# A graph transformer layer on one core: the order of the first loads and of the last steps is changed, and ScalarE normalises the output blocks

## The reference

```python
k = decomp(x, node_type, comp_k, basis_k); q = ...; v = ...      # (n, 8 heads, 16)
kt = einsum('nhi,thij->tnhj', k, relation_att)[edge_type, src]
e = (q[dst] * kt).sum(-1) * relation_pri[edge_type] * 16 ** -0.5
a = softmax of e over the edges of each dst
vt = einsum('nhi,thij->tnhj', v, relation_msg)[edge_type, src]
agg = segment_sum(a[..., None] * vt, dst)
y = relu(decomp(agg, node_type, comp_a, basis_a) + x @ loop_weight + bias)
out = layernorm(x + y)
```

## Time and profile before

| what | us |
|---|---|
| median of 3 runs | 2042.28 |
| lowest, highest | 2038.15, 2045.23 |
| the profiled execution | 2054.15 |
| its span, first to last instruction | 2052.3 |

### The profile page before, as it was taken

One profiled execution on the slowest core, in us unless ns is written; L12 is line 12 of the kernel. 1 busy time (PEld: TensorE's weight loads), 2 busy tenths in 40 slices (PEclk: granted clock), 3 DMA queues, 4 the chain that ended last, 5 costly groups with the idle time before them and its releaser, 6 DMA issues.

```text
span 2052.3 us, 30216 instructions
## 1 busy us (share of the span) xinstructions
PE 1223.7 (60%) x6847; PEld 1015.7 (49%) x6848; DVE 1005.0 (49%) x2888; ACT 789.1 (38%) x2216; POOL 888.9 (43%) x927
## 2 busy tenths in 40 slices
PE   6999428565545555455564565555555455554788
PEld 3445215454445445455454554444544455444678
DVE  5866216444534445344453444434444344453777
ACT  4667216433333333333333333333333333333233
POOL 2781650444454444544445444354443544445000
PEclk9999759666777766777667667667776666667789
DMA  7787530222232222322223222232222322223113
GB/s 228 303 301 313 175 91 12 69 68 75 65 86 73 69 71 63 86 72 67 75 63 85 74 61 77 63 88 67 70 72 65 88 74 61 75 67 85 38 48 106
DMA packets 110628, 194.47 MB, mean 95 GB/s; under 512 B 24345, under 2 KB 76404, under 8 KB 104188
## 3 DMA queue, kind: packets, MB, share of 16 engines
q0 software_dynamic: 41680, 113.71, 19.6%
q1 hardware_dynamic: 66380, 79.10, 11.0%
q10 hardware_dynamic: 2400, 0.07, 0.1%
HBM read 134.12 MB, written 59.48 MB: 94 GB/s over the span
## 4 chain that ended last, share of the span: by engine, by line
another core or an unknown queue 30%; PE 26%; DVE 16%; issue 15%; DVEq 9%; ACT 2%; DMA 1%; ACTq 1%
PE pb L1703 6%; DVE agg L742 5%; PE pb L1651 4%; DVEq L713 4%; PE pb L1538 3%; DVE work L707 3%; PE pb L1813 2%; PE pb L1559 2%; PE pb L1678 2%; PE pb L1609 1%; DVE work L599 1%; PE pb L1640 1%; DVE work L609 1%; DVEq L582 1%
## 5 line engine op out<-in xcount | busy, mean ns | idle before, releaser
L1223 POOL DMA_INDIRECT kv<-table,idx_now x832 | 788.0, 947 | 935.0 <-DVE work L707 645.3
L742 DVE TENSOR_TENSOR agg<-agg,pb 128x136 f32 x832 | 241.8, 291 | 801.5 <-remote 613.8
L1703 PE MATMUL pb<-work,onehot 128*128 128x136 f32 x1664 | 391.6, 377 | 353.4 <-DVE agg L742 225.2
L1703 PEld LDWEIGHTS pb<-work,onehot 128*128 128x128 f32 x1664 | 327.0, 270 | 386.1 <-issue 244.9
L1365 ACT ACTIVATE work<-pb 128x512 f32<-128x512 f32 x208 | 123.9, 596 | 818.9 <-remote 636.6
L1651 PE MATMUL pb<-q_all,work 128*128 x1664 | 313.1, 351 | 0.1
L1651 PEld LDWEIGHTS pb<-q_all,work 128*128 128x128 f32 x1664 | 296.3, 265 | 3.7 <-issue 3.0
L1640 PE MATMUL pb<-ident,onehot 128*128 128x128 f32 x832 | 181.1, 357 | 184.3 <-ACT onehot L1359 99.9
L1352 ACT ACTIVATE work<-lane,neg_lane 128x128 f32<-128x128 f32 x800 | 252.9, 389 | 0.0
L1640 PEld LDWEIGHTS pb<-ident,onehot 128*128 128x128 f32 x832 | 127.6, 184 | 209.6 <-ACT onehot L1359 116.1
L599 DVE TENSOR_TENSOR work<-kv,pb 128x512 f32<-128x512 f32 x208 | 141.9, 682 | 22.0 <-issue 12.0
(11 more groups left out here) (202 smaller groups left out, 1291.4 us busy)
## 6 DMA issues: line engine op xcount, KB each, us to landing
table<-kv SPq DMA_DIRECT2D x49, 1024.0 KB, 4.7
kv<-table,idx_now POOLq DMA_INDIRECT x832
seg<-item_bias SPq DMA_DIRECT2D x52, 64.0 KB
kv<-base_rows SPq DMA_DIRECT2D x7, 448.0 KB, 4.5
kv<-in_x_dram SPq DMA_DIRECT2D x8, 384.0 KB, 5.7
pair<-in_x_dram SPq DMA_DIRECT2D x24, 128.0 KB
base_rows<-pair SPq DMA_DIRECT2D x24, 128.0 KB
onehot<-in_x_dram SPq DMA_DIRECT2D x7, 384.0 KB
```

What stands on the lines that cost most here:

```text
L742: v.tensor_tensor(a, a, PB[banks[i // 2 % len(banks)]][:, (i % 2) * 256:(i % 2) * 256 + W], ALU.add).then_inc(s_added, 1)
L1223: pool.indirect_dma_start(out=kv[:, o:o + 2 * D], out_offset=None, in_=table, in_offset=bass.IndirectOffsetOnAxis(ap=idx_now[par][:, i:i + ...
L1703: mm = t_.matmul(PB[banks[k % len(banks)]][:, u * 256:u * 256 + W], onehot[:, o:o + P], wv[:, b % WR, h * 2 + u, :], start=True, stop=True)
```

## The change

1. **First loads.** SyncE loads the k basis right behind x, ScalarE the v basis as its first instruction. The priorities come as one broadcast load, masked by head (`own_head`, three GpSimd operations) and summed on VectorE, in place of eight loads. GpSimd copies only the destinations first; sources and edge types follow once the bases have landed.
2. **Places in the table stage.** `STARTS_AT` 8 to 9, each column one block later, `QUERIES_AT` from block 45 to 41.
3. **Last group.** Each step of `maxima` stands ahead of two additions, not behind them; `weigh` of batches 2 to 7 is cut into four instructions that alternate with the additions.
4. **Layer stage.** All chunks but the last are normalised on ScalarE, between its copies; VectorE keeps reciprocal and shift, in the middle of `products3`.
5. **Last chunk.** Blocks 0 to 3, 4 and 5, and 6 as three parts, each with its own statistics and root; block 6 gets its own PSUM bank; three stores.

```diff
-        TILES_AT, STARTS_AT, BIAS_AT, QUERIES_AT = 4, 8, 24, BLOCKS - 4
-        COLUMNS_AT = [12, 13, 15, 16, 18, 19, 20]
+        TILES_AT, STARTS_AT, BIAS_AT, QUERIES_AT = 4, 9, 24, BLOCKS - 8
+        COLUMNS_AT = [13, 14, 16, 17, 19, 20, 21]
...
-                dve.wait_ge(s_relations_loaded, 16 * 3 * H)
+                dve.wait_ge(s_own_head, 3)
+                dve.wait_ge(s_relations_loaded, 16 * (2 * H + 1))
+                did(v.tensor_tensor(p3, p3, own_head.unsqueeze(1).broadcast_to([P, T, H]), ALU.mult))
+                did(v.tensor_reduce(pri, p3, AX.X, ALU.add))
...
             for k, steps in enumerate(maxima(g, 1, GROUPS // 2 - 1)):
+                steps()
                 late[2 * k]()
                 late[2 * k + 1]()
-                steps()
...
+                        if between and b == 1:
+                            between()
...
+            def inverse(ch):
                 dve.wait_ge(s_deviation, ch + 1)
                 v.reciprocal(rstd, rstd).then_inc(s_inverse_deviation, 1)
                 dve.wait_ge(s_inverse_deviation, ch + 1)
...
+                v.scalar_tensor_tensor(shift, mv[:, :, 0], -1.0, rstd, ALU.mult, ALU.mult).then_inc(s_shift, 1)
...
+            def stage3(ch, par, first=False):
+                products3(ch + 1, 1 - par, None if first else lambda: inverse(ch - 1))
                 residual(ch, par)
...
              x_chunk(0)
+            sp.dma_start(Bkv[:, :, 0, :], basis_k.rearrange("b (i o) -> i b o", o=D)).then_inc(s_bases_loaded, 16)
...
-            tile_load(0, dst)
-            tile_load(1, src)
-            tile_load(2, edge_type)
+            tile_load(0, dst, s_tile_rows)
...
+            pool.wait_ge(s_bases_loaded, 16 * 2)
+            tile_load(1, src, s_tile_more)
+            tile_load(2, edge_type, s_tile_more)
...
+            def normalise(ch, par, cs):
+                act.wait_ge(s_shift, ch + 1)
+                after(act, s_stored, ch, 16, 0)
+                for c in cs:
+                    a_.activation(yo[:, c * D:(c + 1) * D], y[par][:, c * D:(c + 1) * D], ACT.Identity,
+                                  bias=shift[:, c:c + 1], scale=rstd[:, c:c + 1]).then_inc(s_normalised, 1)
...
+                act.wait_ge(s_normalised, ch * CB)
+                root(0)
+                part(0)
+                root(1)
+                root(2)
+                part(1)
...
+            NORMS = {5: (0, 2), 6: (2, 4), CB: (4, CB)}
+            LAST_NORMS = {3: (0, 2), 4: (2, 4), 5: (4, CB)}
```

More of the change, by code:

```diff
@@ L173, in graph_transformer_layer @@
         pri = w1.take(T)
+        pri_all = w1.take(T * H)
+        own_head = w1.take(H)
         comp = w1.take(4 * NB, 96)
@@ L816, in _ @@
             for b in range(NBATCH):
-                merge(adding(g, range(2 * b, 2 * b + 2), LAST_SBANKS), [lambda: weigh(g, 1, b + 2)] if b + 2 < NBATCH else [])
+                merge(adding(g, range(2 * b, 2 * b + 2), LAST_SBANKS),
+                      [lambda u=u: weigh_item(g, 1, b + 2, u) for u in range(4)] if b + 2 < NBATCH else [])
             dve.wait_ge(s_added, GROUPS * G)
@@ L893, in _ @@
                 stage3(it * 2 + 1, 1)
-            stage3(CHUNKS - 1, 0, final=True)
-            normalise(CHUNKS - 1, 0, range(SPLIT))
+            inverse(CHUNKS - 2)
+            dve.wait_ge(s_shift, CHUNKS - 1)
+            dve.wait_ge(s_normalised, (CHUNKS - 2) * CB)
+            finish(CHUNKS - 1, 0)
         @block.sync
@@ L1054, in store @@
                 hold(sp)
-                last = known(ch) and ch == CHUNKS - 1
-                n = CB - 1 if last else CB
                 oc = yo.rearrange("p (c d) -> p c d", c=CB)
-                sp.dma_start(out[bass.ds(ch * CN, n * P), :].rearrange("(c p) d -> p c d", p=P),
-                             oc[:, 0:n, :]).then_inc(s_stored, 16)
-                if last:
-                    sp.dma_start(out[whole * P:N, :], oc[0:rest, n, :]).then_inc(s_stored, 16)
+                sp.dma_start(out[bass.ds(ch * CN, CN), :].rearrange("(c p) d -> p c d", p=P),
+                             oc[:, :, :]).then_inc(s_stored, 16)
             assert CHUNKS % 2 == 1
@@ L1071, in _ @@
             load(CHUNKS - 1, 0)
-            for ch in range(CHUNKS - 3, CHUNKS):
+            for ch in range(CHUNKS - 3, CHUNKS - 1):
                 store(ch)
-            sp.wait_ge(s_stored, 16 * (CHUNKS + 1))
+            ch, c1 = CHUNKS - 1, LAST_PARTS[0][1]
+            oc = yo.rearrange("p (c d) -> p c d", c=CB)
+            sp.wait_ge(s_normalised, ch * CB + c1)
+            sp.dma_start(out[ch * CN:ch * CN + c1 * P, :].rearrange("(c p) d -> p c d", p=P),
+                         oc[:, 0:c1, :]).then_inc(s_stored, 16)
+            sp.wait_ge(s_normalised, ch * CB + LAST_PARTS[1][1])
+            sp.wait_ge(s_last_normalised, 1)
+            sp.dma_start(out[ch * CN + c1 * P:whole * P, :].rearrange("(c p) d -> p c d", p=P),
+                         oc[:, c1:CB - 1, :]).then_inc(s_stored, 16)
+            sp.dma_start(out[whole * P:N, :], oc[0:rest, CB - 1, :]).then_inc(s_stored, 16)
+            sp.wait_ge(s_stored, 16 * (CHUNKS + 2))
         @block.gpsimd
@@ L1459, in deviation, with finish, root, part @@
                 act.wait_ge(s_mean_var, ch * CB + CB)
+                after(act, s_normalised, ch, CB, 0)
+                hold(act)
                 a_.activation(rstd, mv[:, :, 1], ACT.Sqrt, bias=eps[:, 0:1]).then_inc(s_deviation, 1)
-            def stage3(ch, par, first=False, final=False):
-                for c in range(1, CB):
-                    copy_products(ch, par, c)
-                    if c == 3 and not first:
+            def finish(ch, par):
+                def root(h):
+                    c0, c1 = LAST_PARTS[h]
+                    act.wait_ge(s_mean_var, ch * CB + c1)
+                    a_.activation(rstd[:, c0:c1], mv[:, c0:c1, 1], ACT.Sqrt, bias=eps[:, 0:1])                        .then_inc(s_deviation, 1)
+                def part(h):
+                    act.wait_ge(s_shift, ch + h + 1)
+                    act.wait_ge(s_stored, ch * 16)
+                    for c in range(*LAST_PARTS[h]):
+                        a_.activation(yo[:, c * D:(c + 1) * D], y[par][:, c * D:(c + 1) * D], ACT.Identity,
[6 more added lines that the diff above has]
+                part(1)
@@ L1467, in stage3 @@
+            def stage3(ch, par, first=False, final=False):
+                norms = {} if first else LAST_NORMS if final else NORMS
+                for c in range(1, CB if final else CB + 1):
+                    if c < CB:
+                        copy_products(ch, par, c)
+                    else:
+                        copy_products(ch + 1, 1 - par, 0)
+                    if c == (2 if final else 3) and not first:
                         deviation(ch - 1)
-                if not final:
-                    copy_products(ch + 1, 1 - par, 0)
+                    if c in norms:
+                        normalise(ch - 1, 1 - par, range(*norms[c]))
```

104 lines of the change are left out of this document (72 added, 32 removed).

## The result

| | kernel before | kernel after |
|---|---|---|
| median of 20 timed runs, us | 2043.74 | 2036.94 |
| lowest, highest | 2038.15, 2052.41 | 2029.97, 2044.72 |
| profiled execution | 2054.15 | 2039.78 |
| its span, granted clock | 2052.3, 0.733 | 2038.0, 0.730 |

The ratio is 0.9968, 95% interval 0.9956 to 0.9979: 6.5 us less, 4.3 to 9.0. The forecast was 13.7 less, 2028.6, with 2024 to 2033 as its own range; 2036.94 lies above it. The two profiled executions differ by 14.4, almost the forecast: the one of before lies 10.4 us over its median, that of after 2.8.

What follows compares the result with a forecast made beforehand. No engine is near full, so waits between engines set the end. Gains 5.0 + 5.1 + 2.0 + 1.1 + 0 + 0.5 = 13.7 off the median 2042.28 gave 2028.6 us; own range 2024 to 2033, whole range 2021 to 2039.

Steps and rivals of the forecast that it cites:

- Start: First loads: bases ahead of coefficients gain 3.9, the relation wait 1.5, less 0.4 for two tiny operations; gain 5.0 us.
- Scan: Table stage: scan behind block 9 no longer waits for the `tile_blocks` broadcast; 6.5 less 1.4, gain 5.1 us.
- Blocks 11 to 29: Table stage: columns and item work move by one block while the scan is 5 earlier; nothing late, no term.
- Queries: Query loads at block 41: gathers start up to 3.5 earlier, which shortens the query stage's crawl; gain 2.0 us.
- Last group: Last edge group: earlier steps gain 0.2, weightings alternating with additions 0.9 over six batches; gain 1.1 us.
- Normalising on ScalarE: Layer stage: normalisations fit into ScalarE's slack and nothing waits for VectorE; gain 0.
- Last chunk: End of kernel: last stores go 0.2 later after waiting for chunk 5's store, but fewer bytes stand ahead; gain 0.5 us.
- coefficients take the bases' place: Rival at the start: coefficients queue behind 512 KB, so start gives 1.1 instead of 5.0; 2032.5 us, chance 0.08.
- ScalarE's price: Rival in the layer stage: normalising makes ScalarE the slow side by 5.8 us; 2034.4, chance 0.04.
- the store-bound table stage: Rival: 49 stores bind the table stage, so start and scan gains are lost; 2038.7 us, no change, chance 0.13.
- the late broadcast: Rival at the scan: the broadcast shares engines with stores and its wait comes back whole; 2032.3 us, chance 0.08.
- the output buffer in each chunk: Rival in the layer stage: ScalarE waits for the output buffer, 3.5 in each of five chunks; 2054.0 us, chance 0.07.

Runs made afterwards that it cites:

- coefs_first: The changed kernel with the coefficient loads ahead of the two bases again, bases still ahead of types and relations; ratio to the kernel before 0.9974.
- set A: One-chip set: kernel before again, and it with one part each: new loads and later scan 0.9993, earlier query loads 1.0001, changes behind the edge stage 0.9987.
- D: One-chip set of kernels cut to 6 of 26 edge groups: before 770.75 us, new loads and scan only 760.78, changed 757.19, changed with types ahead and own output buffer 753.17.
- C: One-chip set: kernel before 1380.37 us, changed kernel 1372.56, changed with coefficients and types first and own output buffer: bias terms at block 27 1374.86, at 24 1371.00.
- E: One-chip set repeating two kernels cut to 6 of 26 edge groups: kernel before 576.87 us, changed kernel 568.93.
- Set B: Changed kernel with repairs, ratios to before: bias terms at block 27 0.9950, coefficients first 0.9974, last chunk's own output buffer 0.9960, all three 0.9914.
- group_layer: The kernel before with only the changes to last group, layer stage and last chunk; 2040.91 us, ratio 0.9987.
- start_scan: The kernel before with only the new load order, the scan behind block 9 and columns one block later; 2041.59 us, ratio 0.9993.
- three twins: Profiles with the kernel before's table stage but for query loads: kernel before again, query loads at block 41 (1.0001), only changes behind the edge stage (0.9987).
- long pair: The kernel before and the changed kernel with all 26 edge groups; medians 2043.74 and 2036.94 us, ratio 0.9968.
- short pair: The kernel before and the changed kernel, both cut to 6 of 26 edge groups; 770.75 and 757.19 us, repeated at 576.87 and 568.93.
- before_again: The kernel before, unchanged, profiled a second time; the kernel before took 2043.96 us in that set.
- before_third: The kernel before, unchanged, profiled again in a later set, where it took 1380.37 us.

## Why the prediction was wrong

All profiles together, in the prediction's order. "Unchanged" are the seven profiles with the old loads, "new" those eight with the changed kernel's own order of loads.

*Start, forecast 5.0.* Block 8 at 43.4 to 47.4, mean 45.3, unchanged; 39.6 to 41.8, mean 40.7, new: 4.6 gained, so the sum was nearly right and both its halves wrong. The first projection moves from a mean of 15.1 to 12.4 (2.7, not 3.9), by the coefficients, which land at 8.0 to 10.0 and no more at 6.4 to 6.8: "I take the whole chain 0.5 later" fails; behind the two bases of 256 KB they are 2.3 later in the mean. The wait for the relations, taken as 1.52, is one more draw from a wide range: from the projection to block 8 it takes 28.3 in each new profile, and 27.9 to 32.1 unchanged. The Trainium skill (DMA: Bandwidth & Descriptors, "Issuing engines are not separate DMA queues") states that DMAs run on the same 16 engines and interleave there, whichever engine started them. The traces agree: with the bases ahead of them the coefficients came 2.55 us later in the profile of after, and in coefs_first they are back at 6.66. The page gives no price for it.

*Scan, forecast 5.1.* 8 to 11 takes 10.2 to 16.1, mean 13.2, unchanged, and 10.4 in each new profile: 2.9. The mechanism is right (no new profile waits for the broadcast), the size is not. This is the largest error: the term was taken from one execution in which the wait, 3.67, was the second longest of seven (0.6 to 4.1, mean 2.5). In the profiled pair it is 5.8, which is a main reason why that pair looks like the forecast. In set A start and scan aren't independent either: the two unchanged profiles with block 8 late have a short way from 8 to 11 (46.9 and 11.4, 45.2 and 10.2), the two with it early a long one (43.8 and 16.1, 43.4 and 15.2). Neither gain should be read without the other. Together they move block 11 from a mean of 58.5 to 51.1, 7.4 for the forecast's 10.1, and 6.2 in set A.

*Blocks 11 to 29, forecast 0.* Loss of about 1 us where the item gathers slow the engines (A: 71 for 69; it doesn't show in D, 70.3 and 71.3 for 71.5), 0.3 in C and E. "Nothing is late there" fails.

*Queries, forecast 2.0.* The gathers start 2.2 earlier in every profile (18.3 to about 16.1). To the first group's scan that is worth 1.9 in A (161.0 to 159.0, means of four and two) and 1.0 in D, 1.0 in C, and a loss of 1.6 in E (86.5 and 88.1). Set B's four profiles, 158.8 to 160.9, bring the gain over all profiles at the slower pace down to 1.2 (means of six and eight). That the stage must crawl for the early start to be worth something is plausible, but these numbers don't show it. No stall of ScalarE at block 41.

*Last group, forecast 1.1.* From its scan to the layer stage's first base matmul 36.2 before, 35.5 after, the same in C, D and E: 0.7. By itself, in group_layer, the part gives 1.0, so the term was good; start_scan, which doesn't have it, is 0.4 shorter there as well, which isn't explained. *Normalising on ScalarE, 0:* right; layer stage's TensorE 77.1 and 77.0, with a scatter of 1.4 over all profiles. *Last chunk, 0.5:* 8.5 to 7.4, so 1.1. The late store of chunk 5 was seen rightly, but block 6 by itself and the early stores gain more than taken.

With the means of set A: 3.3 (block 8) + 2.9 - 1.1 + 1.9 + 0.7 + 0.1 + 1.1 = 8.9, at the upper end of the measured 4.3 to 9.0. For C and E the same sum is 5.0 + 2.3 - 0.3 + 0.3 - 0.3 + 1.9 = 8.9, where 7.8 and 7.9 were timed. About 1 us stays open in these two, and 2.4 in A, inside its interval.

So the step that failed is the size of the terms, and the scan's above all: 5.1 stood in the sum, and the runs showed 2.9. In set A, 1.7 are missing at the start and 1.1 are lost between blocks 11 and 29, where the sum had nothing. With the small terms that takes 13.7 to 8.9. Behind it stands the step from one execution to the median: durations came "from that execution, whose 11.9 us over the median lie in it as they do not in the runs", and were then subtracted whole from the median. The profile of before has block 11 at 60.0, its three twins at 57.5 in the mean. These 2.5 are the scan's alone (3.8 later in it, while block 8 came 1.3 earlier). The change removes them, and they can't be gained by runs that don't pay them. The other excess of that profile, the 2.7 of blocks 25 and 26 among it, was no term. What separates 8.9 from the timed 6.5 stays open: scatter, or a part given back at the slower pace.

Of the rivals "coefficients take the bases' place" came true in its mechanism, but not in its price of 3.9. ScalarE's price, the store-bound table stage, the late broadcast and the output buffer in each chunk did not: the earlier trace rows has its answer in 38.6 us of idle time that ScalarE still has, and between 160 and 202 us of the profile after it waited for TensorE alone, never for a table slot. The median, 2036.94, is nearest to the store-bound rival's 2038.7, but by number only: start and scan, which that rival had as lost, are there in every profile.

## What to carry to other kernels

A wait for a transfer that is seen once is a draw from a distribution: before its length is made a term of a sum, look at the same place in two or three more executions, above all when the profiled one lies over the median. When a load is moved to the front, ask for everything behind it when it is needed; here twelve small loads behind 512 KB came 2.3 us later. Where the effect is half a per cent of a long kernel, cut the loops that are not in question and time the short kernel: 40 runs of the long pair left an interval of 4.7 us; in set E ten runs of the short one showed 7.9, with a range of 0.9 for one kernel and 5.8 for the other. But repeat the set: in D the same short pair showed 13.6.

## What the runs showed of the hardware

The same kernel took 2044 to 2081 us in three sets and 1380 in two. The work is the same: VectorE is busy 1005.0 us in the profile of before and 1000.3 in that of before_third, and a gather is 0.95 us in both. What differs is idle time of the engines while GpSimd gathers. GpSimd's gathers in the edge stage, before_again (500 to 1800 us) and before_third (400 to 1200):

```profile
L1223 POOL DMA_INDIRECT kv<-table,idx_now x653 | 620.0, 949 | 680.6 <-DVE work L707 480.2 <-issue 199.8 <-DMA idx_now<-rows_idx 0.6
```

```profile
L1223 POOL DMA_INDIRECT kv<-table,idx_now x638 | 606.1, 950 | 194.4 <-issue 192.6 <-DVE work L707 1.8
```

In the second the gathers follow each other with 0.3 us between them, and set the pace at 39.4 us a group; in the first they wait for VectorE, which is itself idle. The query terms show it best, in stretches of 85 us (before_again, 213 to 298) and 43 us (before_third, 207 to 250):

```profile
L582 DVE SCALAR_TENSOR_TENSOR q_all<-pb,onehot,q_all 128x128 f32 (+1 forms) x42 | 13.7, 348 | 71.9 <-issue 62.3 <-ACT q_all L1312 9.6
```

```profile
L582 DVE SCALAR_TENSOR_TENSOR q_all<-pb,onehot,q_all 128x128 f32 (+1 forms) x131 | 37.0, 345 | 6.3 <-ACT q_all L1312 6.2
```

42 operations in 85 us against 131 in 43. One operation takes the same in both, 348 and 345 ns. The granted TensorE clock of these stretches is 0.64 and 1.00 of full speed, with TensorE busy 25.4 of 85 us and 42.4 of 43; whether the lower clock has any part in the crawl or only follows from an idle TensorE isn't tested. The crawl of the earlier trace rows is thus no property of this program alone; where it is absent, 660 us of this kernel go with it. No experiment tells its cause. Sets D and E bear the same chip number and took 2081.13 and 1380.73, four minutes apart, so the pace doesn't seem to be fixed by the chip. Stages without gathers are nearly the same in all sets: the last group takes 36.2 (35.5 after the change) and the tail 8.5 (7.4) at either pace.
